# K's mask term moved from two TensorE products to a VectorE addition, and the maximum's subtraction to GpSimd

## What is computed

```python
xn = _ln(x, ln_w, ln_b)
q = xn @ Wq + bq
k = xn @ Wk + bk + (1.0 - src_mask) * -1000000.0
q = softmax(q.reshape(b, t, h, dh), axis=-1)
k = softmax(k.reshape(b, t, h, dh), axis=1)       # over the 64 tokens of a sequence
v = ((xn @ Wv + bv) * src_mask).reshape(b, t, h, dh)
att = einsum('bnhd,bnhl->bhdl', k, v)
y = einsum('bnhd,bhdl->bnhl', q, att).reshape(b, t, d)
hh = _ln(y, ln2_w, ln2_b) * (1.0 + scale) + shift  # scale, shift: silu(cond) @ W_emb + b_emb
hh = silu(hh) @ W_out + b_out
return x + hh
```

## Time and profile before

| | us |
|---|---|
| median of 3 runs (lowest to highest) | 335.39 (332.82 to 336.79) |
| profiled execution: its time | 336.49 |
| profiled execution: its span | 334.7 |
| TensorE busy | 315.3 (94%) |
| TensorE weight loads busy | 269.0 (80%) |
| VectorE busy | 277.3 (83%) |
| GpSimd busy | 198.3 (59%) |
| ScalarE busy | 182.7 (55%) |
| TensorE's mean granted clock | 0.985 of full |
| distance of 512-column product starts, up to 21.4 us and after | 0.43 and 0.23 |
| moved by transfers | 19.68 MB; SyncE's and ScalarE's queues 18.5% of the transfer engines' time |

### The profile page before, as it was taken

The page is one execution under the profiler, slowest core; times in us unless marked ns, Lnnn a source line. Parts: engine busy times, 40 slices in busy tenths (PEclk is TensorE's granted clock), DMA queues, the critical chain, the costliest instruction groups (busy, mean ns, idle before and its releaser), DMA issues.

```text
span 334.7 us, 14404 instructions
## 1 busy us (share of the span) xinstructions
PE 315.3 (94%) x5644; PEld 269.0 (80%) x5644; DVE 277.3 (83%) x749; ACT 182.7 (55%) x360; POOL 198.3 (59%) x261
## 2 busy tenths in 40 slices
PE   3999999999999999999999999999999999998736
PEld 1478777988879898988888898989898888988625
DVE  3695888989898989989897979799898989886771
ACT  1327574566484755565574847565556648454240
POOL 2305137767766775767677667757676775747420
PEclk9999999999999999999999999999999999999896
DMA  7702010040404021030304040210304010101011
GB/s 238 256 0 66 20 47 4 2 129 2 127 5 118 7 66 59 11 115 0 125 0 125 0 125 0 71 55 25 101 0 125 0 63 0 66 4 63 4 66 63
DMA packets 19418, 19.68 MB, mean 59 GB/s; under 512 B 817, under 2 KB 18865, under 8 KB 19394
## 3 DMA queue, kind: packets, MB, share of 16 engines
q1 hardware_dynamic: 18144, 17.96, 17.2%
q10 hardware_dynamic: 1250, 1.39, 1.3%
HBM read 10.95 MB, written 8.39 MB: 58 GB/s over the span
## 4 chain that ended last, share of the span: by engine, by line
PE 87%; DVE 5%; POOL 3%; DMA 2%; issue 1%; ACT 1%; SPq 0%; POOLq 0%; DVEq 0%
PE bv L674 29%; PE bk L674 28%; PE by L674 13%; PE by L734 4%; PE by L745 4%; PE by L777 4%; PE by L724 4%; DMA q_t<-in_wv 2%; POOL y_s L350 1%; DVE ystat L647 1%; DVE y_s L640 1%; POOL yr L345 1%; DVE z_s L565 0%; DVE q_s L557 0%; DVE rq L636 0%
## 5 line engine op out<-in xcount | busy, mean ns | idle before, releaser
L408 ACT ACTIVATE k_t<-k_t 128x512 f32<-128x512 f32 x32 | 20.2, 632 | 55.9 <-DVE k_t L591 55.9
L243 POOL TENSOR_TENSOR h_lo<-h_s,h_hi 128x512 fp32r<-128x512 f32 x30 | 38.1, 1290 | 10.0 <-ACT h_hi L434 10.0
L239 POOL TENSOR_TENSOR z_s<-z_s,mod_shift 128x512 f32<-128x512 f32 x30 | 30.7, 1043 | 21.6 <-DVE z_s L565 21.6
L674 PE MATMUL bv<-w_o_hi,h_hi 128*128 128x256 f32 x128 | 35.1, 295 | 4.5 <-ACT h_hi L434 4.5
L358 POOL TENSOR_TENSOR x_all<-x_all,bo_all 128x1024 f32 (+1 forms) x16 | 38.3, 2396 | 0.0
L391 ACT ACTIVATE xt_hi<-by 128x512 fp32r<-128x512 f32 x32 | 17.5, 595 | 37.1 <-PE by L745 37.1
L587 DVE TENSOR_REDUCE kmax<-bk 128x8 f32<-128x512 f32 x32 | 22.0, 687 | 16.2 <-PE bk L674 16.2
L350 POOL TENSOR_SCALAR y_s<-y_s,yr 128x256 f32<-128x256 f32 x62 | 33.8, 558 | 2.6 <-POOL yr L347 2.2
L345 POOL TENSOR_TENSOR yr<-yr,neg_half 128x4 f32<-128x4 f32 x16 | 16.2, 1012 | 31.4 <-DVE yr L654 31.4
L674 PE MATMUL bv<-w_o_lo,h_hi 128*128 128x256 f32 x128 | 34.7, 292 | 0.0
L440 ACT ACTIVATE xhat<-x_all,xr 128x256 f32 (+1 forms) x64 | 33.1, 590 | 2.3 <-POOL xr L333 2.3
(11 more groups left out here) (106 smaller groups left out, 857.6 us busy)
## 6 DMA issues: line engine op xcount, KB each, us to landing
x_all<-in_x SPq DMA_DIRECT2D x16, 512.0 KB, 4.5
out<-x_all SPq DMA_DIRECT2D x15, 512.0 KB, 3.2
z_s<-in_w_emb ACTq DMA_DIRECT2D x1, 512.0 KB, 8.6
h_s<-in_w_emb ACTq DMA_DIRECT2D x1, 512.0 KB, 10.5
out<-x_all SPq DMA_DIRECT2D x2, 256.0 KB, 2.1
y_s<-in_wk SPq DMA_DIRECT2D x1, 256.0 KB, 3.3
q_t<-in_wq SPq DMA_DIRECT2D x1, 256.0 KB, 5.5
th<-in_cond_t ACTq DMA_DIRECT2D x1, 256.0 KB, 7.2
```

The lines of the kernel that those rows point to most:

```text
L239: return eng.tensor_tensor(z, z, mod_shift[:, c, span(g, GB)].unsqueeze(2).broadcast_to([P, GB, SEQ]), ALU.add)
L243: return eng.tensor_tensor(h_lo[:, c, :], h_s[:, c, :], h_hi[:, c, :].bitcast(fp32), ALU.subtract)
L408: nc.scalar.activation(k_t[:, par, c, :], k_t[:, par, c, :], ACT.Exp).then_inc(kexp_d, 1)
L674: return nc.tensor.matmul(dst, lhsT, rhs, start=start, stop=stop)
```

## The change

K's mask term leaves TensorE. A new SBUF tile `off` (two buffers of 128 x 512 fp32) receives the group's mask row broadcast to all partitions by a transfer on SyncE's queue, one per group; ScalarE turns it into 1 - mask (`mask_offset`, at the end of its list). VectorE's first pass over a bank of K is now a `scalar_tensor_tensor` that computes off x -1000000 + bank and writes `k_t`; its second pass takes the maximum from `k_t` in SBUF. GpSimd subtracts the maximum from `k_t` in place (`k_shifted`): half 0 first thing in its list, half 1 behind the two `h_low`. ScalarE's exponential of half 1 moves from ahead of `q_t` to the end of its list, behind V tile 3. TensorE's first two products of a bank wait for the first half of `xt_hi` alone, the next two for the second. `n_all`, `mask_r`, `pick` and `sel`, and what fills them, are gone.

```diff
+        off = sb("off", [P, 2, GT])
...
+            def load_off(g, parity):
+                sp.dma_start(off[:, parity, :].unsqueeze(1),
+                             mask_g[span(g, 1)].unsqueeze(0).broadcast_to([P, 1, GT])).then_inc(off_in[parity], 16)
+
             sp.dma_start(w_k, wk.rearrange("(c p) n -> p c n", p=P)).then_inc(wk_in, 16)
             load_x(0, 0)
+            load_off(0, 0)
             sp.dma_start(w_qv[:, :, 0:D], wq.rearrange("(c p) n -> p c n", p=P)).then_inc(wqv_in, 16)
...
             load_x(1, 1)
+            load_off(1, 1)
...
                     wait(sp, xstat_d, 4 * i)
                     load_x(i + 1, 1 - par)
+                    wait(sp, kadd_d, 2 * i)
+                    load_off(i + 1, 1 - par)
                 if O and not (isinstance(i, int) and i < 3):
                     store(i - 3)
...
-            pool.memset(n_all[:, :].bitcast(fp32), 0.0).then_inc(n_zero, 1)
-            pool.wait_ge(pool_init, 2)
-            nc.gpsimd.tensor_tensor(pick[:, :], ident[:, 0:G], ident[:, 32:32 + G], ALU.add).then_inc(pick_d, 1)
...
-            def select(g, parity):
...
+            def k_shifted(g, parity, c):
+
+                wait(pool, kmax_d, 2 * g + c + 1)
+                kk = k_t[:, parity, c, :].rearrange("p (b s) -> p b s", s=SEQ)
+                nc.gpsimd.tensor_tensor(kk, kk, kmax[:, c, :].unsqueeze(2).broadcast_to([P, GB, SEQ]),
+                                        ALU.subtract).then_inc(ksub_d, 1)
 
             def body(i, par, N, F, B, O):
+                if F:
+                    k_shifted(i, par, 0)
...
-                    select(g, 1 - par)
...
                         h_low(nc.gpsimd, c).then_inc(hlo_d, 1)
+                if F:
+                    k_shifted(i, par, 1)
...
-            act.dma_start(mask_r[0:G, :], mask_rows.rearrange("(g b) s -> g (b s)", b=GB)).then_inc(mask_in, 16)
...
+            def mask_offset(g, parity):
+
+                wait(act, off_in[parity], 16 * (g // 2 + 1) if isinstance(g, int) else 8 * (g - parity) + 16)
+                nc.scalar.activation(off[:, parity, :], off[:, parity, :], ACT.Identity, scale=-1.0,
+                                     bias=1.0).then_inc(off_d, 1)
...
                 if F:
-                    for c in range(C):
-                        wait(act, ksub_d, 2 * i + c + 1)
-                        nc.scalar.activation(k_t[:, par, c, :], k_t[:, par, c, :], ACT.Exp).then_inc(kexp_d, 1)
+                    wait(act, ksub_d, 2 * i + 1)
+                    nc.scalar.activation(k_t[:, par, 0, :], k_t[:, par, 0, :], ACT.Exp).then_inc(kexp_d, 1)
...
                     v_tile(i, par, 2)
                     v_tile(i, par, 3)
+                    wait(act, ksub_d, 2 * i + 2)
+                    nc.scalar.activation(k_t[:, par, 1, :], k_t[:, par, 1, :], ACT.Exp).then_inc(kexp_d, 1)
+                if N:
+                    mask_offset(i + 1, 1 - par)
...
                         wait(dve, k_d, 2 * i + c + 1)
-                        wait(dve, ksub_d, 2 * i + c - 1)
-                        kk = bk_[c][:, :].rearrange("p (b s) -> p b s", s=SEQ)
-                        nc.vector.tensor_reduce(out=kmax[:, c, :], in_=kk, axis=AX.X, op=ALU.max).then_inc(kmax_d, 1)
-                        wait(dve, kmax_d, 2 * i + c + 1)
+                        wait(dve, off_d, i + 1)
                         if c == 0:
                             wait(dve, ekt_d, 2 * i - 2)
-                        nc.vector.tensor_tensor(k_t[:, par, c, :].rearrange("p (b s) -> p b s", s=SEQ), kk,
-                                                kmax[:, c, :].unsqueeze(2).broadcast_to([P, GB, SEQ]),
-                                                ALU.subtract).then_inc(ksub_d, 1)
+                        nc.vector.scalar_tensor_tensor(k_t[:, par, c, :], off[:, par, :], -1000000.0, bk_[c][:, :],
+                                                       ALU.mult, ALU.add).then_inc(kadd_d, 1)
+                        wait(dve, kadd_d, 2 * i + c + 1)
+                        wait(dve, ksub_d, 2 * i + c - 1)
+                        nc.vector.tensor_reduce(out=kmax[:, c, :],
+                                                in_=k_t[:, par, c, :].rearrange("p (b s) -> p b s", s=SEQ),
+                                                axis=AX.X, op=ALU.max).then_inc(kmax_d, 1)
...
-                    wait(pe, ksub_d, 2 * i + t - 1)
+                    wait(pe, kadd_d, 2 * i + t - 1)
...
-                            pe.wait_ge(n_ready, 2)
                             pe.wait_ge(weights_ready, 1)
-                        if c == 0:
-                            wait(pe, sel_d, i + 1)
-                        mm(bk_[c][:, :], sel[:, par, :], n_all[:, :], True, False)
-                        wait(pe, hi_d, 2 * i + 2)
                         for j in range(C):
-                            mm(bk_[c][:, :], w_k_hi[:, j, out_c], xt_hi[:, j, :], False, False)
+                            wait(pe, hi_d, 2 * i + j + 1)
+                            mm(bk_[c][:, :], w_k_hi[:, j, out_c], xt_hi[:, j, :], j == 0, False)
```

More of the change, by code:

```diff
@@ L63, in build_layer @@
         mod_shift = sb("mod_shift", [P, C, BATCH])
-        n_all = sb("n_all", [P, GT], f32r)
-        pick = sb("pick", [P, G])
-        sel = sb("sel", [P, 2, P], f32r)
+        off = sb("off", [P, 2, GT])
         neg_half = sb("neg_half", [P, T])
@@ L131, in build_layer @@
         brow_in = sem("brow_in")
-        mask_in = sem("mask_in")
+        off_in = [sem("off_in0"), sem("off_in1")]
         wk_in = sem("wk_in")
@@ L138, in build_layer @@
         we_in = sem("we_in")
-        n_zero = sem("n_zero")
-        pick_d = sem("pick_d")
-        sel_d = sem("sel_d")
+        off_d = sem("off_d")
+        kadd_d = sem("kadd_d")
         x_in = [sem("x_in0"), sem("x_in1")]
@@ L246, in build_layer @@
         o_h = out.rearrange("(g t p) d -> g p t d", t=T, p=P)
+        mask_g = mask_rows.rearrange("(g b) s -> g (b s)", b=GB)
         def group_of(tensor, g):
```

20 lines of the change are left out of this document (2 added, 18 removed).

## The result

The changed kernel takes **340.19 us** (median of 4 runs, 338.56 to 341.45), the kernel before on the same chip 334.73 (4 runs, 332.82 to 336.79): ratio 1.0141, 95% interval 1.0097 to 1.0185. The forecast was 330.7, with a range up to 335.0. It was wrong in sign: 5.5 us slower instead of 4.7 faster. Medians are of all runs of a kernel; ratios and pooled medians leave out those that took over 1.5% longer than its fastest.

What follows compares the result with a forecast made beforehand. TensorE was taken as the bound, busy 94% of the span. Start +0.2, steps 1 and 2 +0.2 and steps 3 to 15 -5.1 gave -4.7 us: from 335.39 to 330.7 us, range 327.5 to 335.0.

Steps and rivals of the forecast that it cites:

- Term 3: Start of the kernel: the broadcast transfer ahead of Wq and Wv makes Wv 1.0 us late, costing +0.2 us.
- term 1: Steps 3 to 15: mask products gone, less a low-word wait of mean 0.08, gain 0.39 us each, 5.1 in all.
- term 2: Steps 1 and 2: ScalarE's added work delays `xt_hi` and so TensorE, together +0.2 us.
- VectorE, GpSimd, ScalarE in full steps: Full loop steps: the work added on these three engines stays hidden, cost 0.
- VectorE becomes the bound: Rival, loop: VectorE's new pass at half rate, +0.7 us per step, kernel at 345 us; chance 0.07.
- nothing is gained by an unseen wait in the loop: Rival: an unseen wait replaces the removed products, time stays 335.4 us; chance 0.08.
- slower: Whole kernel: slower than before by more than about 1% (3.35 us); chance 0.10.
- the start costs more: Rival, start: Wv 1.4 us late and the clock's rise with it, +1.5 us instead of +0.2, 332.0; chance 0.1.

Runs made afterwards that it cites:

- e4: The kernel before plus only the changed kernel's two broadcast mask transfers at the start, their tile never used: 339.55 us, ratio 1.0127.
- g2: The changed kernel with 18 already-met waits added ahead of TensorE's loop: 336.48 us, ratio 1.0038.
- e9: e6 with `off` at the end of SBUF and unused tiles in the places of the removed ones: 334.55 us, ratio 0.9968.
- h1: e9 with 30 short waits on TensorE in place of 18: 331.43 us, ratio 0.9893.
- g1: The same kernel as e6, built and run once more: 332.93 us, ratio 0.9941.
- e1: The kernel before without its 32 mask products, the mask left out of K, all else kept: 333.22 us, ratio 0.9943.
- e2: The changed kernel with the first two broadcast mask transfers moved behind the weights in SyncE's queue: 335.14 us, ratio 1.0006.
- e3: The changed kernel with GpSimd's bias sum in step 0 waiting until VectorE has made the modulation: 338.56 us, ratio 1.0080.
- e5: The changed kernel with e2's moved transfers and e3's held-back bias sum: 334.04 us, ratio 0.9936.
- g4: The same kernel as e5, built and run once more: 333.71 us, ratio 0.9955.
- e7: e1 with 17 short waits added on TensorE: 332.75 us, ratio 0.9932.
- e6: The changed kernel with e2's transfers, e3's wait and g2's eighteen waits: 331.05 us, ratio 0.9886.
- g3: e6 with 60 short waits in place of 18: 337.31 us, ratio 1.0059.

## Why the prediction was wrong

The sum, by medians: the transfers alone +4.6 (e4), the gap +3.7 (g2 against the changed kernel), the loop -0.26 x 13 = -3.4: +4.9, where +5.5 was measured (+4.7 by the ratio). The terms are less sure than the total: by their ratios the first is 3.0 to 5.5 and the second 1.5 to 5.3.

- **Term 3, the start, failed most: +0.2 forecast, +4.6 measured by e4.** The step of the argument that fell is the choice between two bounds, 0.76 us by all transfer engines' rate and 1.4 by the queue's own. Neither was an upper bound: Wv came 3.7 us late. The bytes of a broadcast are not the bytes of a weight: beside it the full transfer engines moved 229 GB/s instead of 317 (e4), which explains about half of the delay. Why, and what the other half is, no run shows. The 4.6 holds some of the next item as well: step 1 is 1.15 us longer in e4's trace. A forecast from rates of the 512 KB and 256 KB loads had no row of such a transfer at the head of a full queue. Its second half, that half of what the slow pace costs would be given back, is not borne out as a size: the profiled pair has all of the 2.49 us back in step 0, the median of e4 none. When the pace rises differs from execution to execution, and that is luck.
- **The low words' wait (term 1): right.** 0.03 and 0.13 us per step measured, 0.03 and 0.12 forecast. The size of the gain per step was short by a third, for a reason absent from the sum: 0.08 us in the output products, which e9 and h1 show to be SBUF placement, and some issue time every second step. No rival had it.
- **Steps 1 and 2 (term 2): the mechanism right, a neighbour missed.** With the bias sum held back (g1) step 1 is 15.22 us, +0.35 where +0.45 was forecast, and the chain names the reason, `off` on ScalarE (0.62 us) between V and `xt_hi`. In the changed kernel itself this lies under something larger, +1.73: VectorE's `mod_scale` held for 2.28 us. Most of that is not the change's: e1 and e4, without its code, have step 1 at 15.79 and 16.02 when step 0 is short; the changed kernel, e2 and g2 have 16.33 to 16.60. The 0.3 to 0.8 us between are the change's share. 0.3 of it is `emb`, held beside `k_shifted` (0.58 to 0.61 us in seven profiles of the new code, 0.28 in the kernel before). GpSimd's `k_shifted` of half 1 (1.05 us) stands ahead of the bias sum in step 0 and pushes it further into VectorE's modulation, where `sel` (0.29) stood. I had listed what is queued behind the subtractions for full steps, and not for step 0. Here the Trainium skill, page GPSIMD Engine Reference, section Specifications, says that GpSimd shares SBUF interfaces with VectorE and contends with VectorE instructions in a 2-port performance mode or with two SBUF inputs. The trace agrees as far as it goes: `mod_scale` has one tensor from SBUF and the long operation of GpSimd's beside it ends 0.09 us before it does. Whether `mod_scale` runs in such a mode no row shows.
- **VectorE, GpSimd, ScalarE in full steps: cost 0, right.** h1, which has all of the new passes, has a step of 18.01 us, and e1, which has none of them and its tiles in the same places, 18.08. So the rivals *VectorE becomes the bound* and *nothing is gained by an unseen wait in the loop* both fall. The pass that reads the bank and the offset tile takes 682 ns, so the half rate that the rival gave it did not come.
- **Not in any rival: the gap of 1.97 us in step 15.** It turns up wherever mask products leave TensorE's list at the old code position (e1, e2, e3, e5, g4 and the changed kernel), always with 25 products left; g2 removes it with 18 idle waits. The transfers of code on queue 8 show what it is: TensorE goes on 2.4 to 2.7 us after one has started that comes 7 us later in the step than in the kernels without the gap. The forecast took TensorE's list to run without a break wherever no semaphore holds it, and had no term for this. A page's words fit, in part: the Trainium skill, page Runtime: NRT & Kernel Launch, section Instruction fetch mechanics, says that instructions come in blocks of 256, prefetched in sequence, and that a taken branch to outside the window costs a fetch. Counted in TensorE's instructions in program order, the loop's body once (two for a small product, as e7's shift of nine products by 17 waits also gives), the gaps of steps 4, 15 and 16 in the changed kernel stand about 768 apart, three such blocks, and the packets of queue 8 have 16 KB. But the late load starts in straight code, 9 us behind the loop's last branch (283.5 us), and what the rule does not give is why e9 has the gap and e6, with the same list, has not.
- **The chances.** 0.5 for the forecast and 0.1 for slower left almost no room for a loss outside the loop. The rival *the start costs more* was the right place, priced at +1.5; the one that would have gone to the other side stood on VectorE.

**What stays open.** What decides whether the code behind the loop is loaded as the loop ends or 7 us later. The count of instructions has a part in it (g2, g3, h1), but e6 and e9 differ in SBUF addresses alone. Why the gap's price differs is open in part: step 15 takes 21.5 to 21.9 us where the granted clock falls behind the gap (the changed kernel, e2, e3, e9, g4), and 20.2 to 20.6 where it does not (e1, e5, e7), but in the medians the price is 1.1 us (e5 and g4 against e6 and g1, give or take 1.0) or 3.7 (the changed kernel against g2, 1.5 to 5.3 by the ratios). With 1.1 the sum above would be +2.3, and the missing 3 us would have no owner.

**The better kernel.** With the transfers behind the weights, the bias sum held back, the tiles at their old places and 30 idle waits (h1) the change is worth three quarters of what the forecast had said of it, 3.5 us of the 4.7: 331.43 against 334.95 (six runs; the ratio's interval leaves 2.0 to 5.2). e6 (331.05 and, repeated, 332.93) lies beside it. The idle waits are a matter of luck with the code's position and not a design.

## What to carry to other kernels

The price of taking work off the bounding engine was right to 0.13 us per step (0.39 forecast, 0.26 measured), and the time was lost in three places that run once: price the head of the queue, the first steps and the code behind a loop as carefully as the step that repeats. A transfer put ahead of one that starts the chain is to be priced by a row of its own kind (a broadcast of one row is not a weight matrix) or moved behind. When a profile shows TensorE standing with "issue" as the reason, look in the view of transfers for a packet of the kind "instruction" just ahead of the gap's end before you look for the cause in the data. Idle instructions can move such a gap, but g3 shows that they can also make a worse one.

## What the hardware showed that I had not expected

- A broadcast load of one 2 KB row to 128 partitions (262 KB) ahead of two weight loads delays the second of them by 3.7 us (9.00 to 12.68), about five times the 0.76 us of its bytes at 343 GB/s. TensorE's products for Wv start at 12.7 to 13.0 us in the changed kernel, e4 and g2 and at 14.3 in e3, at 9.05 in the kernel before. The transfer engines, full in both, move 229 GB/s and not 317 meanwhile (e4, 4 to 8 us).
- A one-input VectorE operation on 128x128 that takes 0.27 to 0.29 us takes 2.28 when it begins inside a 2.4 us GpSimd addition, and one on 128x256 takes 1.88 instead of 0.28 (e4), 2.02 in e1.
- TensorE can stand for 1.9 to 2.5 us in straight code behind a loop, and goes on 2.4 to 2.7 us after a 16 KB transfer of the kind "instruction" has started. The loop itself (six turns of some 1440 instructions, as the trace counts them) needs none after its first turn. In five of the eight traces with this gap the granted clock fell behind it (0.66 over the next 5 us in the changed kernel, twelve products in 4.55 us instead of 3.01), and step 15 cost 3.2 to 3.6 us more than the 18.3 of the kernel before; in the other three it stayed at full, and step 15 cost 1.9 to 2.3 more.
- The same 24 products take 2.80 or 2.88 us by where tiles lie in SBUF.
- A maximum over 64 takes as long from SBUF as from a bank (686 and 687 ns).
- Two executions of one start differ by 2.4 us in step 0 (14.3 in e1, 16.8 in the kernel before) by when the fast pace of TensorE sets in, at about 14 us or at 21, and step 1 takes part of it back, because VectorE then meets GpSimd's bias sum.
